# Ranking tokens within their experts by sums over fours of token tiles instead of single tiles

## The chip, the cores and the metric

The kernel runs on one NeuronCore of a Trainium2 chip. The metric is the device time of one execution in microseconds (us), as the median of the runs. The engines are TensorE (PE: matrix products; its weight loads are listed apart as PEld), VectorE (DVE), ScalarE (ACT), GpSimd (POOL) and SyncE (SP), which issues most DMA transfers. Each runs its own instructions in order and waits for others through semaphores.

## The reference

Two layers work on 64 batches of 64 tokens with 1024 features (4096 tokens), each with a residual sum. The first multiplies each batch by one of 16 small matrices and adds a routed low-rank term over 8 experts. The second, cut to what matters:

```
w = weight[adapter_ids];  y = einsum('bij,bkj->bik', x, w)        # a 1024 x 1024 adapter for each batch
base_out = y @ base_w.T + base_b
res_hidden = y @ A.T                                              # 64 wide
logits = y @ router_w.T;  probs = softmax(logits)                 # 16 experts
topw, topi = top_k(probs, 2);  topw = topw / (sum(topw) + 1e-6)
combine = sum(one_hot(topi, 16) * topw)
delta = einsum('bse,bsr,eor->bso', combine, res_hidden, B)
x = x + base_out + delta * 0.5
```

Each token takes two of the 16 experts. The kernel computes an expert's product only for the tokens that chose it, so it must sort the 8192 (token, choice) pairs by expert. The place of a pair within its expert is a count of the tokens ahead of it that chose the same expert.

## The kernel before

Tokens lie on 128 partitions in NT = 32 token tiles of 128 tokens (two batches each). Matrix products in fp32 are written as three products of operands split into a high and a low part (`split_product`, lines 1437 to 1441).

The second layer has these stages. First come the adapter products with `w` (lines 1538 to 1571), which also leave the router logits and the 64-wide hidden values in DRAM. Then comes the base product for each token tile, `base_part(t, n)` (line 1575): 16 parts a tile, three products of 512 columns each, with `xp_hi` and `xp_lo` as weights and `base_hi` and `base_lo` as moving operand. One tile's `xp_hi` and `xp_lo` are kept at a time, in four quarters. ACT makes a quarter of `xp_hi` (`y_high`, line 795) when PE has used that quarter of the tile before, and DVE makes the same quarter of `xp_lo` (`y_low`, line 1174) behind it. The order of everything is written out by hand, in one list for each engine.

The routing lies among the first eight base tiles. DVE picks the two experts of each token in `choose_first` and `choose_second` (lines 1197 to 1217). The result is `hot`, 128 tokens x 32 tiles x 16 experts, 1 where the token chose the expert, and `hot_sum`, its sum over the tiles. The semaphore `hot_ready` says that both are there.

After base tile 2, PE runs `rank_sums` (line 1595). All its products add into one PSUM bank of 512 columns (32 tiles x 16 experts). The first, with the strictly triangular matrix `before`, counts the tokens ahead within the same tile. The other 31, with the matrix `ones`, add the whole count of tile t to all later tiles: tile 0 to 31 tiles (496 columns), tile 1 to 30, and so on to 16 columns. A last product of 16 columns sums `hot_sum` over the partitions. It sets `sums_done`.

DVE then weighs the choices (`weigh`), turns the counts into slots (`place`, line 1230, which waits for `sums_done`) and makes the one-hot table `hot_a` (`tile_of_rows`, line 1254) and `hot_b` (`row_of_rows`, line 1261). PE uses these in `row_sums` beside base tile 6 to find each slot's token. POOL gathers the hidden values by those rows, and the expert products follow, mixed with base tiles 8 to 12. The remaining base tiles come after that, with the gathers of the expert results, the final sums and the stores.

DVE's list around the ranking is: `y_low` for tile 2, quarters 2 and 3; `choose_second`; `y_low` for tile 3, quarters 0 and 1; four subtractions of expert weights (`expert_low(6)` and `(7)`, line 1187); `y_low` for tile 3, quarters 2 and 3; `weigh`; the four quarters of tile 4; `place`; the four of tile 5; `tile_of_rows`.

Of the kernel before, what the change touches and what calls it, by code (L numbers as in the profile page):

```python
# [6 lines left out]
F32 = mybir.dt.float32  # L7
F32R = mybir.dt.float32r
# [3 lines left out]
AX = mybir.AxisListType  # L12

P = 128
# [3 lines left out]
E0, R0 = 8, 16  # L18
E1, R1 = 16, 64
# [5 lines left out]
GT = GR // P  # L25
# [8 lines left out]
NT = NB // 2  # L34
# [53 lines left out]
def bcast(ap, axis, n):  # L88
    shape = list(ap.shape)
    shape.insert(axis, n)  # L90
    return ap.unsqueeze(axis).broadcast_to(shape)


def build(nc, xT, id0, id1, w0, p0T, rb0, b0T, w1T, baseT, q1T, bias1, out):
# [6 lines left out]
    ctx = ExitStack()  # L101
    with ctx:
# [3 lines left out]
        def sb(stack, name, shape, dt=F32):  # L106
            return stack.enter_context(nc.sbuf_tensor(name, shape, dt))
# [12 lines left out]
        ones = sb(ctx, "ones", [P, P], F32R)  # L120
# [4 lines left out]
        desc0 = sb(ctx, "desc0", [P, GT, E0])  # L125
        desc1 = sb(ctx, "desc1", [P, E1])
        rbias = sb(ctx, "rbias", [P, E0])
        sm = sb(ctx, "sm", [P, 10, GT, E0])
        sv = sb(ctx, "sv", [P, 8, GT])
        tok = sb(ctx, "tok", [P, NT])  # L130
        gate = sb(ctx, "gate", [P, 2, NT])
        slots = sb(ctx, "slots", [P, 2 * NT], I32)
        rows = sb(ctx, "rows", [P, NX], I32)
# [45 lines left out]
        with ExitStack() as s:  # L179
            lg = sb(s, "lg", [P, NT, E1])  # L180
            rt = sb(s, "rt", [P, 6, NT, E1])
            hot = sb(s, "hot", [P, NT, E1], F32R)
            hot_sum = sb(s, "hot_sum", [P, E1], F32R)
            etab_f = sb(s, "etab_f", [1, NX])
            rv = sb(s, "rv", [P, 9, NT])
            ev = sb(s, "ev", [P, 5, E1])
# [11 lines left out]
        def bank(i, n=1):  # L198
            return psum[:, i * 512:(i + n) * 512]
# [684 lines left out]
        def _(dve):  # L884
# [305 lines left out]
            rl = Chain(dve, route_chain)  # L1190
# [16 lines left out]
            def choose_second():  # L1207
                dve.reduce_max(m2, sh2, AX.X).then_inc(shift2, 1)
                dve.wait_ge(shift2, 1)
                rl(tt(tmp, sh2, bcast(m2, 2, E1), ALU.is_equal))  # L1210
                rl(tt(tmp, tmp, rank, ALU.mult))
                rl(dve.reduce_max(k2, tmp, AX.X))
                rl(tt(oh2, rank, bcast(k2, 2, E1), ALU.is_equal))
                rl(tt(hot[:, :, :], oh1, oh2, ALU.add))
                with nc.allow_low_precision("small whole numbers"):
                    dve.reduce_sum(hot_sum[:, :], hot[:, :, :].bitcast(F32).rearrange("p t e -> p e t"), AX.X
                                   ).then_inc(hot_ready, 1)

            def weigh():
# [84 lines left out]
            y_low(2, 2)  # L1304
            y_low(2, 3)
            choose_second()
            y_low(3, 0)
            y_low(3, 1)
# [86 lines left out]
            for i in range(LAST + 1):  # L1395
                t = KEPT + i
# [12 lines left out]
        def _(pe):  # L1409
            mm = pe.matmul  # L1410
# [184 lines left out]
            def rank_sums():  # L1595


                pe.wait_ge(hot_ready, 1)
                mm(bank(0), before[:, :], hot[:, :, :].rearrange("p t e -> p (t e)"), start=True, stop=False,
                   skip_group_check=True)  # L1600
                for t in range(NT - 1):
                    mm(bank(0)[:, (t + 1) * E1:NT * E1].rearrange("p (t e) -> p t e", e=E1), ones[:, :],
                       bcast(hot[:, t, :], 1, NT - 1 - t), start=False, stop=t == NT - 2, skip_group_check=True)
                mm(bank(1)[:, 0:E1], ones[:, :], hot_sum[:, :], start=True, stop=True).then_inc(sums_done, 1)

            def row_sums(n):
# [20 lines left out]
            def expert_of(s):  # L1627
                return pe.value_load(etab[0:1, s:s + 1], min_val=0, max_val=E1 - 1)
# [21 lines left out]
            for t in range(FIRST):  # L1650
                for n in range(16):
                    base_part(t, n)
                    if t == 0 and n == 1:
                        turn(total)
                    if t == 0 and n == 5:
                        rh_of(total)
                    if t == FIRST - 2 and n % 2 == 1:
                        row_sums(n // 2)
                    if t == FIRST - 1 and n == 13:
                        turn_hw(0)  # L1660
                if t == 2:
                    rank_sums()
            pe.wait_ge(etab_ready, 1)
            pe.wait_ge(exp_lo_done, E1)
            e = expert_of(0)
            for s in range(NX):
                expert(s, e)
                if s + 1 < NX:
                    e = expert_of(s + 1)
# [50 lines left out]
```

## Time and profile before

| | us |
|---|---|
| median of 3 runs | 1165.05 |
| lowest, highest | 1164.32, 1165.34 |
| the profiled execution's own time | 1167.17 |
| its span in the trace | 1165.6 |
| PE busy | 1103.1 (95% of the span) |
| DVE busy | 686.3 (59%) |
| ACT busy | 505.3 (43%) |
| POOL busy | 222.2 (19%) |

The span runs from the first to the last instruction in the trace. The profiled execution took 1.6 us more than its span and 2.1 us more than the median. Products on PE are pipelined: the record of one overlaps that of the next, so what a product costs in a row of them is the distance from its start to the start of the next, not its duration.

### The profile page before, as it was taken

Reading aid. Unit: us, or ns where it says so; the run is one execution under the profiler, and the core shown is the slowest. Engines: PE = TensorE matmul, PEld = TensorE weight load, DVE = VectorE, ACT = ScalarE, POOL = GpSimd, SP = SyncE. Lnnn points to the kernel's source line nnn. Section 1 sums busy time; section 2 is a strip of 40 time slices with the busy share of each in tenths; the row PEclk is TensorE's granted clock in tenths of the full one; section 3 lists DMA queues with packets and bytes.
Section 4 is the critical chain, followed back from the end, with each engine's and each line's share of the span. In section 5 each row is a group of like instructions: output and inputs, shape, how many; then the busy total and the mean of one; then the engine's idle time right before and its main releaser. Section 6 shows DMA issues by size and latency. Waiting matters only on the chain.

```text
span 1165.6 us, 22333 instructions
## 1 busy us (share of the span) xinstructions
PE 1103.1 (95%) x5801; PEld 916.3 (79%) x5802; DVE 686.3 (59%) x1321; ACT 505.3 (43%) x1027; POOL 222.2 (19%) x354
## 2 busy tenths in 40 slices
PE   4899979999999899999999999999999999999998
PEld 4899967878778687878878878767777778888886
DVE  4788943563755637463565486834455366566666
ACT  1012213563745637453565462134555444444443
POOL 1111110020201102010111000054545232223210
PEclk9899979999999899999999999999999999999999
DMA  6499765493765729475665432169999899999995
GB/s 212 169 313 326 258 223 177 136 323 114 256 222 195 266 82 325 153 259 180 221 221 183 137 102 88 57 223 330 345 336 334 315 404 341 348 354 337 324 323 204
DMA packets 114925, 283.11 MB, mean 243 GB/s; under 512 B 17202, under 2 KB 22322, under 8 KB 112946
## 3 DMA queue, kind: packets, MB, share of 16 engines
q1 hardware_dynamic: 85232, 178.95, 43.3%
q0 software_dynamic: 29216, 102.91, 26.0%
q10 hardware_dynamic: 418, 0.53, 0.2%
q8 instruction: 28, 0.46, 0.2%
q14 instruction: 31, 0.25, 0.1%
HBM read 181.65 MB, written 100.70 MB: 242 GB/s over the span
## 4 chain that ended last, share of the span: by engine, by line
PE 74%; DVE 11%; issue 4%; DMA 4%; ACT 3%; DVEq 1%; SPq 1%; ACTq 1%; POOL 0%; POOLq 0%; another core or an unknown queue 0%
PE psum L1439 18%; PE psum L1441 17%; PE psum L1440 17%; PE psum L1533 3%; PE psum L1637 3%; PE psum L1636 3%; PE psum L1525 2%; PE psum L1645 2%; DVE x1g L1045 2%; PE psum L1534 2%; PE psum L1551 2%; PE psum L1553 1%; DMA xp<-act_scratch 1%; PE psum L1449 1%; ACT w L821 1%
## 5 line engine op out<-in xcount | busy, mean ns | idle before, releaser
L1439 PE MATMUL psum<-base_hi,xp_hi 128*128 128x512 f32 x512 | 207.6, 405 | 6.2 <-DVE xp_lo L1177 3.4
L1441 PE MATMUL psum<-base_hi,xp_lo 128*128 128x512 f32 x512 | 200.4, 391 | 0.0
L1440 PE MATMUL psum<-base_lo,xp_hi 128*128 128x512 f32 x512 | 200.2, 391 | 0.0
L1439 PE MATMUL psum<-w,xp_hi 128*128 128x512 f32 x448 | 182.8, 408 | 6.3 <-DVE xp_lo L1095 3.2
L1441 PE MATMUL psum<-w,xp_lo 128*128 128x512 f32 x448 | 177.7, 397 | 0.0
L1440 PE MATMUL psum<-w,xp_hi 128*128 128x512 f32 x448 | 177.3, 396 | 0.0
L1077 DVE TENSOR_TENSOR w<-raw,w 128x1024 fp32r<-128x1024 f32 x112 | 132.4, 1221 | 29.5 <-ACT w L758 23.6
L639 POOL DMA_DIRECT2D raw<-w1T x112 | 59.4, 530 | 442.8 <-DVE w L1077 417.5
L803 ACT ACTIVATE xp_hi<-xp 128x256 fp32r<-128x256 f32 x124 | 51.6, 418 | 183.1 <-PE psum L1441 152.3
L1439 PEld LDWEIGHTS psum<-base_hi,xp_hi 128*128 128x128 f32 x512 | 96.2, 188 | 39.8 <-issue 15.6
L1177 DVE TENSOR_TENSOR xp_lo<-xp,xp_hi 128x256 fp32r<-128x256 f32 x124 | 51.9, 424 | 119.3 <-ACT xp_hi L803 96.5
L1441 PEld LDWEIGHTS psum<-base_hi,xp_lo 128*128 128x128 f32 x512 | 96.1, 188 | 20.8
L647 POOL DMA_INDIRECT hwn<-rh_scratch,rows x80 | 76.0, 951 | 184.3 <-DVE rows L1274 115.8
L1440 PEld LDWEIGHTS psum<-base_lo,xp_hi 128*128 128x128 f32 x512 | 96.4, 188 | 16.8
L1439 PEld LDWEIGHTS psum<-w,xp_hi 128*128 128x128 f32 x448 | 84.4, 188 | 26.8 <-issue 9.2
L758 ACT ACTIVATE w<-raw 128x1024 fp32r<-128x1024 f32 x104 | 104.6, 1052 | 0.0
L1441 PEld LDWEIGHTS psum<-w,xp_lo 128*128 128x128 f32 x448 | 84.3, 188 | 20.5
L1440 PEld LDWEIGHTS psum<-w,xp_hi 128*128 128x128 f32 x448 | 84.7, 189 | 17.8
L868 ACT ACTIVATE x1t<-x1t,bias 128x128 f32<-128x128 f32 x256 | 78.6, 390 | 12.7 <-DMA x1t<-act_scratch 12.7
L1095 DVE TENSOR_TENSOR xp_lo<-xp,xp_hi 128x512 fp32r<-128x512 f32 x58 | 40.0, 690 | 70.9 <-ACT xp_hi L710 70.5
L1109 DVE COPY yp<-psum 128x512 f32 x28 | 19.4, 691 | 96.2 <-PE psum L1441 95.9
L720 ACT ACTIVATE yp<-psum 128x512 f32 x28 | 16.8, 599 | 136.1 <-PE psum L1441 135.9
(278 smaller groups left out, 1993.5 us busy)
## 6 DMA issues: line engine op xcount, KB each, us to landing
raw<-w1T POOLq DMA_DIRECT2D x120, 512.0 KB, 5.6
delta_scratch<-dl SPq DMA_DIRECT2D x80, 512.0 KB
xp<-act_scratch SPq DMA_DIRECT2D x74, 256.0 KB, 3.3
act_scratch<-yT SPq DMA_DIRECT2D x72, 256.0 KB, 2.2
act_scratch<-x1g SPq DMA_DIRECT2D x16, 1024.0 KB, 5.3
x1t<-act_scratch SPq DMA_DIRECT2D x64, 256.0 KB
out<-x1t SPq DMA_DIRECT2D x62, 256.0 KB
xg<-xT SPq DMA_DIRECT2D x15, 1024.0 KB, 8.6
```

The lines of the kernel that those rows point to most:

```text
L639: pool.dma_start(raw[:, i, :], w1T[bass.ds(a, 1), i, :, :].rearrange("a p k -> p (a k)")).then_inc(raw_in[i], 16)
L647: pool.indirect_dma_start(hwn[s % HRING][:, :], None, rhs[0:NB, :, :].rearrange("b c z -> (b c) z"), bass.IndirectOffsetOnAxis(ap=rows[:, ...
L758: act.activation(w_hi[:, i, :], raw[:, i, :], ACT.Copy).then_inc(w_hi_done, 1)
L803: act.activation(xp_hi[:, ks, :].rearrange("p i (b c) -> p b i c", b=2), xp[:, t % 2, :, ks, :], ACT.Copy).then_inc(yh_done, 1)
L868: last = act.activation(x[:, :, i, :], x[:, :, i, :], ACT.Identity, bias=bias[:, i:i + 1])
L1077: tt(w_lo[:, i, :], raw[:, i, :], w_hi[:, i, :].bitcast(F32), ALU.subtract).then_inc(w_lo_done, 1)
L1095: tt(xp_lo[:, ks, :].rearrange("p i (b c) -> p b i c", b=2), xp_of(j, total, ks), xp_hi[:, ks, :].bitcast(F32).rearrange("p i (b c) -> p b ...
L1177: tt(xp_lo[:, ks, :].rearrange("p i (b c) -> p b i c", b=2), xp[:, t % 2, :, ks, :], xp_hi[:, ks, :].bitcast(F32).rearrange("p i (b c) -> ...
L1439: mm(out, a_hi, b_hi, start=start, stop=False, skip_group_check=True)
L1440: mm(out, a_hi, b_lo, start=False, stop=False, skip_group_check=True)
L1441: return mm(out, a_lo, b_hi, start=False, stop=stop, skip_group_check=True)
L1533: mm(rh_ps, yq_hi[:, i, :], q2[:, i, :], start=i == 0, stop=False, skip_group_check=True)
```

## The change

`rank_sums` now goes by fours of tiles. Three products, each over all eight fours at once, add a tile's count to the tiles d = 1, 2 and 3 places on within its four: they read 8 pieces of 48, 32 or 16 columns out of `hot` and write 8 such pieces with gaps between them. Seven products add the count of a whole four to all later tiles: 448, 384 and so on down to 64 columns. The count of a four, `hot_four` (128 x 8 x 16), comes from a new DVE reduction of `hot`, and `hot_sum` is now reduced from `hot_four` in place of `hot`. The temporary tile `sm` of the first layer (10 x 2 x 8 words of 4 bytes for each partition, 640 bytes) now shares its place with tiles that are written later, so the buffers allocated after it lie 640 bytes lower.

```diff
-        sm = sb(ctx, "sm", [P, 10, GT, E0])
         sv = sb(ctx, "sv", [P, 8, GT])
         tok = sb(ctx, "tok", [P, NT])
+        with ExitStack() as s:
+            sm = sb(s, "sm", [P, 10, GT, E0])
         gate = sb(ctx, "gate", [P, 2, NT])
...
             hot = sb(s, "hot", [P, NT, E1], F32R)
+            hot_four = sb(s, "hot_four", [P, NT // 4, E1], F32R)
...
                 rl(tt(hot[:, :, :], oh1, oh2, ALU.add))
                 with nc.allow_low_precision("small whole numbers"):
-                    dve.reduce_sum(hot_sum[:, :], hot[:, :, :].bitcast(F32).rearrange("p t e -> p e t"), AX.X
+                    rl(dve.reduce_sum(hot_four[:, :, :], hot[:, :, :].bitcast(F32).rearrange(
+                        "p (b i) e -> p b e i", i=4), AX.X))
+                    dve.reduce_sum(hot_sum[:, :], hot_four[:, :, :].bitcast(F32).rearrange("p b e -> p e b"), AX.X
                                    ).then_inc(hot_ready, 1)
...
-                for t in range(NT - 1):
-                    mm(bank(0)[:, (t + 1) * E1:NT * E1].rearrange("p (t e) -> p t e", e=E1), ones[:, :],
-                       bcast(hot[:, t, :], 1, NT - 1 - t), start=False, stop=t == NT - 2, skip_group_check=True)
+                fours = NT // 4
+                out = bank(0).rearrange("p (b i e) -> p b i e", i=4, e=E1)
+                for d in range(1, 4):
+                    mm(out[:, :, d:4, :].rearrange("p b i e -> p b (i e)"), ones[:, :],
+                       hot[:, :, :].rearrange("p (b i) e -> p b (i e)", i=4)[:, :, 0:(4 - d) * E1],
+                       start=False, stop=False, skip_group_check=True)
+                for b in range(fours - 1):
+                    mm(bank(0)[:, (b + 1) * 4 * E1:NT * E1].rearrange("p (t e) -> p t e", e=E1), ones[:, :],
+                       bcast(hot_four[:, b, :], 1, (fours - 1 - b) * 4), start=False, stop=b == fours - 2,
+                       skip_group_check=True)
```

The order of PE's instructions before, at the start of `rank_sums` behind base tile 2 (the row gives line, operation, output and inputs, columns, and the semaphore waited for):

```order
L1441 MATMUL psum<-base_hi,xp_lo 128x512
L1599 MATMUL psum<-hot,before 128x512 [waits hot_ready]
L1602 MATMUL psum<-hot,ones 128x496
L1602 MATMUL psum<-hot,ones 128x480
L1602 MATMUL psum<-hot,ones 128x464
L1602 MATMUL psum<-hot,ones 128x448
L1602 MATMUL psum<-hot,ones 128x432
L1602 MATMUL psum<-hot,ones 128x416
```

The list of L1602 goes on in steps of 16 columns down to 16. The same place on PE in the changed kernel, whole, up to the first product of base tile 3:

```order
L1603 MATMUL psum<-hot,before 128x512 [waits hot_ready]
L1608 MATMUL psum<-hot,ones 128x8x48
L1608 MATMUL psum<-hot,ones 128x8x32
L1608 MATMUL psum<-hot,ones 128x8x16
L1612 MATMUL psum<-hot_four,ones 128x448
L1612 MATMUL psum<-hot_four,ones 128x384
L1612 MATMUL psum<-hot_four,ones 128x320
L1612 MATMUL psum<-hot_four,ones 128x256
L1612 MATMUL psum<-hot_four,ones 128x192
L1612 MATMUL psum<-hot_four,ones 128x128
L1612 MATMUL psum<-hot_four,ones 128x64
L1615 MATMUL psum<-hot_sum,ones 128x16
```

Ten products stand where 31 stood. The product ahead of them and the one behind them are the same as before.

DVE before, from the making of `hot` to `weigh`:

```order
L1214 TENSOR_TENSOR hot<-rt 128x512 [waits route_chain]
L1216 TENSOR_REDUCE hot_sum<-hot 128x16 [waits route_chain]
L1177 TENSOR_TENSOR xp_lo<-xp,xp_hi 128x2x2x64 [waits yh_done] x2
L1187 TENSOR_TENSOR w<-raw,w 64x1024 [waits exp_hi_done] x4
L1177 TENSOR_TENSOR xp_lo<-xp,xp_hi 128x2x2x64 [waits yh_done] x2
L1223 TENSOR_REDUCE rv<-rt 128x32 [waits exp1]
```

The same place on DVE in the changed kernel:

```order
L1216 TENSOR_TENSOR hot<-rt 128x512 [waits route_chain]
L1218 TENSOR_REDUCE hot_four<-hot 128x128 [waits route_chain]
L1220 TENSOR_REDUCE hot_sum<-hot_four 128x16 [waits route_chain]
L1179 TENSOR_TENSOR xp_lo<-xp,xp_hi 128x2x2x64 [waits yh_done] x2
L1189 TENSOR_TENSOR w<-raw,w 64x1024 [waits exp_hi_done] x4
L1179 TENSOR_TENSOR xp_lo<-xp,xp_hi 128x2x2x64 [waits yh_done] x2
```

One reduction more stands ahead of `hot_ready` and of all that follows on DVE. Nothing else moved.

## Rows read from the trace of the kernel before

**Rows 1.** The page: busy time, share of the span and instructions of each engine

```profile
PE 1103.1 (95%) x5801; PEld 916.3 (79%) x5802; DVE 686.3 (59%) x1321; ACT 505.3 (43%) x1027; POOL 222.2 (19%) x354
```

**Rows 2.** Busy time of each engine in stretches of the span

```profile
core 0: us, PE busy (x) PEld busy (x) DVE busy (x) ACT busy (x) POOL busy (x), PEclk, DMA share, GB/s
698.00:703.10 5.10, 5.10 (x36) 4.82 (x35) 4.98 (x6) 2.03 (x5) 0.00 (x0) 1.00 0.26 103
758.00:870.00 112.00, 108.22 (x473) 79.78 (x472) 51.88 (x98) 52.69 (x106) 59.01 (x62) 1.00 0.87 306
870.00:1165.60 295.60, 286.36 (x1381) 233.24 (x1379) 175.65 (x267) 131.58 (x379) 79.98 (x82) 1.00 0.92 330
```

**Rows 3.** The chain that ended last, 696 to 740 us: start, us, what

```profile
698.67 4.40 PE psum L1602 x31
...
724.83 0.24 PE psum L1441
...
725.97 5.41 DVE hot_a L1255
```

**Rows 4.** Timeline of PE: start, us, engine, line, operation, shape

```profile
698.28 0.39 PE L1599 MATMUL psum<-hot,before 128*128 128x512 f32 x1
698.51 4.56 PE L1602 MATMUL psum<-hot,ones 128*128 128x496 f32 x31
702.93 0.26 PE L1604 MATMUL psum<-hot_sum,ones 128*128 128x16 f32 x1
703.04 0.48 PE L1439 MATMUL psum<-base_hi,xp_hi 128*128 128x512 f32 x1
```

**Rows 5.** The same timeline in four narrow windows within L1602

```profile
699.98 0.33 PE L1602 MATMUL psum<-hot,ones 128*128 128x384 f32 x1
...
701.21 0.40 PE L1602 MATMUL psum<-hot,ones 128*128 128x256 f32 x2
...
702.07 0.37 PE L1602 MATMUL psum<-hot,ones 128*128 128x128 f32 x2
...
702.48 0.38 PE L1602 MATMUL psum<-hot,ones 128*128 128x64 f32 x2
```

**Rows 6.** Groups of DVE reductions by shape, 695 to 725 us: busy, mean ns

```profile
L1216 DVE TENSOR_REDUCE hot_sum<-hot 128x16 fp32r<-128x512 f32 x1 | 1.0, 1014 | 0.0
...
L1212 DVE TENSOR_REDUCE rv<-rt 128x32 f32<-128x512 f32 x1 | 0.7, 687 | 0.0
...
L1243 DVE TENSOR_REDUCE ev<-rt 128x16 f32<-128x256 f32 x1 | 0.4, 420 | 0.0
```

**Rows 7.** Timelines of DVE and of PE's weight loads around the ranking

```profile
696.76 1.01 DVE L1216 TENSOR_REDUCE hot_sum<-hot 128x16 fp32r<-128x512 f32 x1
...
698.05 0.19 PEld L1599 LDWEIGHTS psum<-hot,before 128*128 128x128 f32 x1
...
703.48 0.76 DVE L1177 TENSOR_TENSOR xp_lo<-xp,xp_hi 128x256 fp32r<-128x256 f32 x2
...
725.54 0.42 DVE L1177 TENSOR_TENSOR xp_lo<-xp,xp_hi 128x256 fp32r<-128x256 f32 x1 [1.22 <-ACT xp_hi L803]
```

**Rows 8.** Timeline where PE waits for DVE ahead of base tile 6

```profile
736.88 1.43 DVE L1177 TENSOR_TENSOR xp_lo<-xp,xp_hi 128x256 fp32r<-128x256 f32 x4
737.41 0.19 PEld L1439 LDWEIGHTS psum<-base_hi,xp_hi 128*128 128x128 f32 x1 [1.91 <-ACT nat L812]
...
737.76 0.39 PE L1440 MATMUL psum<-base_lo,xp_hi 128*128 128x512 f32 x1
```

**Rows 9.** Timeline of PE in the first layer, products of plain f32

```profile
96.44 2.02 PE L1449 MATMUL psum<-p,xg 128*128 128x136 f32 x16
98.20 0.37 PE L1439 MATMUL psum<-h_hi,b_hi 128*128 128x256 f32 x1
```

**Rows 10.** The page: two of its costliest groups on PE

```profile
L1440 PE MATMUL psum<-base_lo,xp_hi 128*128 128x512 f32 x512 | 200.2, 391 | 0.0
...
L1440 PE MATMUL psum<-w,xp_hi 128*128 128x512 f32 x448 | 177.3, 396 | 0.0
```

## The prediction

> **What bounds the kernel now.** I read the page's busy times first. PE is busy for 95% of the span, DVE for 59% [rows 1], so PE work that disappears can count fully, and DVE work only where PE waits for it. Next I asked for busy time by stretches. In the 5.1 us of the ranking PE never stands still, at a granted clock of 1.00; behind it PE is busy for 108.2 of 112 and 286.4 of 295.6 us, while the DMA engines are at 0.87 and 0.92 [rows 2]. Then I read the chain that ended last. It runs through all 31 products of L1602 as one piece of 4.40 us, stays on PE to the end of base tile 4 (724.83), and only then goes to DVE for `hot_a` [rows 3]. So the ranking products are on the path. Last came the timelines, for the price of a product by its size [rows 4, 5] and for how close DVE is behind or ahead [rows 7, 8].
>
> The products as a whole: the first of L1602 starts at 698.51 and the product behind the last at 702.93, 4.42 us for 31 products and 7936 columns [rows 4]. That is 0.143 us each. The new list has 10 products and 2560 columns, a third of both, but the price of a product isn't proportional to its columns, so I split it by size.
>
> **The price by size.** From start to start [rows 4, 5]:
> - 496 to 400 columns (7 products, mean 448): 699.98 - 698.51 = 1.47 us, 0.21 each.
> - 384 to 272 (8, mean 328): 701.21 - 699.98 = 1.23, 0.154 each.
> - 256 to 144 (8, mean 200): 702.07 - 701.21 = 0.86, 0.108 each.
> - 128 to 80 (4): 0.41, 0.10 each. 64 to 16 (4): 702.93 - 702.48 = 0.45, 0.11 each.
>
> So below some 200 columns nothing gets cheaper: a product costs 0.11 us however small. Above it the price rises to 0.21 at 448. I read off between the bands 0.18 at 384, 0.15 at 320, 0.13 at 256, and 0.11 for 192, 128 and 64.
>
> **What the change adds on PE.** The seven products over fours (448 down to 64 columns): 0.21 + 0.18 + 0.15 + 0.13 + 3 x 0.11 = 1.00 us. The three products over d have 8 x 48 = 384, 256 and 128 columns: 0.18 + 0.13 + 0.11 = 0.42 us. Together 1.42 us in place of 4.42: **3.00 us less on PE**.
>
> This takes the three as if they wrote one piece. They write eight pieces of 48, 32 or 16 columns with gaps, and no product of the kernel before does so. The lower bound is 0.42 us. For the upper I take the dearest product per column that the trace has: 16 records of L1449 (8 products of plain f32, two records each) take 98.20 - 96.44 = 1.76 us [rows 9], 0.22 us for 136 columns, 1.62 ns a column. By that 768 columns would cost 1.24 us, 0.82 more. I take the lower value: within a piece the columns lie side by side, the operand types are those of L1602, and L1602 itself reads its moving operand in pieces of 16 columns at the prices above.
>
> The Trainium skill speaks against this (SBUF — State Buffer, section "Door 1: The DMA port swizzle"): it states that PSUM has lines of 8 bytes and that any access to it that isn't contiguous slows matmuls significantly. It gives no factor, and no row here shows such a product. Were each of the three doubled, the sum would be 0.42 us worse.
>
> **What it adds on DVE.** The reduction L1216 took 1.01 us, while one of the same 512 elements that reads them side by side took 0.69 and one of 256 took 0.42 [rows 6]. That is 0.15 fixed and 0.54 for 512 elements read in order; read 16 words apart, 0.15 and 0.86. The new reduction to `hot_four` reads 512 elements, again 16 words apart inside each sum: 1.01 us, and 0.69 at the least. The one to `hot_sum` now reads 128: 0.15 + 0.86 / 4 = 0.37 us, at the least 0.15 + 0.14 = 0.29, at the most 1.01 as before. The instruction gap adds about 0.04. So `hot_ready` comes later by 1.01 + 0.04 + 0.37 - 1.01 = 0.41 us, with bounds of 0.01 and 1.05.
>
> The Trainium skill has a rule for this as well (same page and section): SBUF works in lines of 16 bytes, and a step to a new line at each element costs extra. The trace agrees, 1.01 against 0.69 us [rows 6]. By the rule `hot_four` costs the 1.01 that I take; by the length of the sums alone it would be 0.69, and the wait worked out next would vanish.
>
> **The wait that this makes.** `hot_sum` was done at 696.76 + 1.01 = 697.77 [rows 7]. PE loaded its weights for L1599 at 698.05. From the end of a DVE instruction to a weight load that waits for it takes 0.11 us: the first `xp_lo` of the four ends at 736.88 + 0.42 = 737.30 and the load starts at 737.41 [rows 8]. So the data was usable at 697.88, with a cover of 0.17 us. Now it is usable at 698.29. After such a stall the second product starts 0.35 behind the weight load (737.41 to 737.76) [rows 8], that is at 698.64, where it started at 698.51 [rows 4]. The stall is **0.13 us**; by the bounds of the reductions it is 0 to 0.77 (usable at 698.93, second product at 699.28). Behind the waiting product in PE's queue stands all of base tile 3, so the stall counts fully.
>
> **What is late next.** Base tile 3 would start at 703.04 - 2.87 = 700.17. Its first two quarters of `xp_lo` come just behind the reductions on DVE, by 698.9: in time. Its third quarter stands behind four subtractions of expert weights. It started at 703.48 [rows 7], now 0.41 later, lasts 0.42 and is usable 0.11 behind: 704.42. PE wants it two quarters into the tile, 24 products of 0.23 us [rows 4] after the start: 705.6. Cover 1.2 us. So this limits the gain only above some 4.0 us. `weigh` ends some 0.4 us later, by 706.5, and nothing on PE needs it. `place` waits for `sums_done`, long set, and starts behind the last quarter of tile 4, which moves with PE. DVE stands idle for 1.22 us ahead of 725.54 and is released there by ACT behind PE [rows 7], so the long `hot_a` (5.41 us, on the path [rows 3]) starts earlier by the whole gain too. The wait of PE for DVE at 737.41 [rows 8] starts and ends with the same chain and stays as it is. Row table, gathers, expert products and stores all start behind it.
>
> The smaller move: `hot_four` and the 640 bytes by which the buffers shift. I cost them at nothing: the DMA sizes, queues and counts stay the same.
>
> **The sum.** 3.00 - 0.13 = 2.87 us. The profiled execution, 1167.17 us with a span of 1165.6, would become 1164.3 with a span of 1162.7. The runs' median stands 2.1 us lower at 1165.05 and becomes **1162.2 us**, 0.25% less. What a measurement of this kernel can tell from no change is about 0.2%, here 2.3 us, so the forecast lies just over that.
>
> **Rivals.**
> - *The gap-writing products and the wait are dear.* The three products at 1.62 ns a column give 0.82 us back, a wait at its upper bound 0.64 more. Gain 2.05 with the first alone, 1.4 with both: 1163.0 to 1163.6 us, within 0.2%. For it: no row shows such a write, and the page cited has a rule against it. Against: both bounds are far from the nearest rows.
> - *The gain is given back later.* PE is idle for 3.8 + 9.2 = 13 us from 758 on, with the DMA engines at 0.87 to 0.92 [rows 2]. If an earlier start only meets transfers that end when they did, and these waits grow by 2 us, the time is 1164.2. For it: the DMA share. Against: every transfer of these stretches is released by the chain that moves.
> - *Slower by the layout.* `base_hi`, `base_lo`, `xp` and `raw` lie 640 bytes lower; `w` stays. Products of one form cost differently by where they read: records of 391 ns with `base`, 396 with `w` [rows 10]. If the shift costs each of the 1536 base products (3 x 512) those 5 ns, that is 7.7 us: 1165.05 - 2.87 + 7.7 = 1169.9. It eats the gain from 1.9 ns a product on and is slower by over 0.2% from 3.4 ns on. Against: nothing ties the 5 ns to the address rather than to what else ran then.
> - *The products aren't fewer.* The order of instructions shows 10 in place of 31, so this has no chance worth giving.
>
> **How the numbers follow.** Forecast (gain 2.4 to 3.3) 0.62; dear writes or wait 0.15; given back 0.17; layout 0.06. The forecast lies near the limit of 0.2% and the runs spread by 0.5 us to each side, so 0.05 of its 0.62 counts as "same", and 0.03 of the first rival as "faster". Faster 0.57 + 0.03 = 0.60; same 0.05 + 0.12 + 0.17 = 0.34; slower 0.06. The range goes from 1161.3 (full 3.0 and a low median) to 1164.2 (most of the gain given back).
>
> **What would show it.** In the changed profile: ten products between L1603 and L1615 with about 1.4 us from the first start to L1615's; the three of L1608 at 0.18, 0.13 and 0.11 from start to start (the first rival: 0.2 us and more each); two reductions of 1.0 and 0.37 us and a weight load of L1603 that starts 0.1 us behind the second; base tile 3 some 2.9 us earlier, and `hot_a` too; PE's idle time from then on the same 13 us (more in the second rival); the 512-column records of the base products at 391 ns (the third: 396). The prediction is wrong if the 2.9 us at tile 3 don't arrive, or if they do and the end doesn't move with them.

## The result, and the profile after

The changed kernel takes 1159.72 us (median of 19 runs, 1155.03 to 1164.31); the kernel before, run alongside, 1164.32 us (19 runs, 1160.98 to 1168.26). The ratio is 0.9958 with a 95% interval of 0.9945 to 0.9972: 4.9 us less, between 3.3 and 6.4. The forecast was 2.9 us less, so the direction is right and the gain is 2.0 us too small. The time lies below the range that I gave (1161.3 to 1164.2).

Read first the stretch that the change touches. The page after, busy time of each engine (as rows 1):

```profile
PE 1100.2 (95%) x5780; PEld 913.8 (79%) x5781; DVE 686.6 (59%) x1322; ACT 504.1 (43%) x1027; POOL 221.4 (19%) x354
```

PE is busy for 2.9 us less with 21 instructions less [rows 1]. The timeline of DVE, PE's weight loads and PE around the ranking, after (as rows 4 and 7: start, us, engine, line, operation):

```profile
698.87 1.06 DVE L1218 TENSOR_REDUCE hot_four<-hot 128x128 fp32r<-128x512 f32 x1
699.96 0.37 DVE L1220 TENSOR_REDUCE hot_sum<-hot_four 128x16 fp32r<-128x128 f32 x1
...
700.39 0.19 PEld L1603 LDWEIGHTS psum<-hot,before 128*128 128x128 f32 x1 [0.28 <-DVE hot_sum L1220]
700.39 0.50 PE L1603 MATMUL psum<-hot,before 128*128 128x512 f32 x1
...
700.73 0.52 PE L1608 MATMUL psum<-hot,ones 128*128 128x384 f32 x3
...
701.08 1.14 PE L1612 MATMUL psum<-hot_four,ones 128*128 128x448 f32 x7
...
702.05 0.26 PE L1615 MATMUL psum<-hot_sum,ones 128*128 128x16 f32 x1
...
702.16 0.48 PE L1443 MATMUL psum<-base_hi,xp_hi 128*128 128x512 f32 x1
```

From the first product of the ranking to that of `hot_sum` it was 702.93 - 698.28 = 4.65 us [rows 4]; now it is 702.05 - 700.39 = 1.66. That is 2.99 us less, and every profile of the study with the new products has 1.65 to 1.67, every one with the old 4.65 to 4.69.

This stretch begins 2.11 us later on the clock (700.39 against 698.28), which the change did not cause: in this execution the first loads landed 0.9 us later, and more of the early work fell into stretches of half clock. So everything below is compared with the ranking's own start, or between many profiles, and the total by the medians of the runs. The busy times in stretches (columns as in rows 2), after:

```profile
core 0: us, PE busy (x) PEld busy (x) DVE busy (x) ACT busy (x) POOL busy (x), PEclk, DMA share, GB/s
700.40:702.10 1.70, 1.70 (x13) 1.64 (x12) 1.67 (x3) 1.53 (x4) 0.00 (x0) 1.00 0.00 0
758.00:870.00 112.00, 109.42 (x481) 81.28 (x480) 53.33 (x100) 53.93 (x108) 59.89 (x64) 1.00 0.88 316
870.00:1161.90 291.90, 282.89 (x1370) 231.09 (x1368) 174.15 (x265) 129.48 (x377) 77.72 (x80) 1.00 0.92 329
```

PE stands still for 2.6 + 9.0 = 11.6 us from 758 on, where it was 13.0 [rows 2]. The chain that ended last, after, around the ranking and on to the one-hot tables (start, us, what):

```profile
700.53 0.36 PE psum L1603
700.89 0.35 PE psum L1608 x3
701.24 0.97 PE psum L1612 x7
...
723.95 0.24 PE psum L1445
...
725.09 5.41 DVE hot_a L1259
```

DVE's timeline just ahead of it, after:

```profile
724.66 0.43 DVE L1179 TENSOR_TENSOR xp_lo<-xp,xp_hi 128x256 fp32r<-128x256 f32 x1 [1.22 <-ACT xp_hi L805]
```

`hot_a` starts at 725.09 where it was 725.97 [rows 3]. That is 0.88 us earlier although the ranking began 2.11 later: the 2.99 us arrive whole, and DVE is idle ahead of it for the same 1.22 us [rows 7]. So the forecast held up to here, and some 1.9 us of the gain come from somewhere else. The page's groups don't show where. After:

```profile
L1445 PE MATMUL psum<-base_hi,xp_lo 128*128 128x512 f32 x512 | 200.0, 391 | 0.0
L1444 PE MATMUL psum<-base_lo,xp_hi 128*128 128x512 f32 x512 | 199.9, 390 | 0.0
...
L1444 PE MATMUL psum<-w,xp_hi 128*128 128x512 f32 x448 | 177.8, 397 | 0.0
L1445 PE MATMUL psum<-w,xp_lo 128*128 128x512 f32 x448 | 177.5, 396 | 0.0
```

Almost nothing moves here [rows 10]: a record holds a product's whole pass, 0.39 us, while the next one starts 0.23 us later. What counts on a full PE is the distance from start to start. I took it from the trace for every pair of neighbouring 512-column products outside the stretches of half clock and call it the spacing. Means in ns, some 1,250 to 1,300 pairs in the adapter stage, 800 in the last base stage, 190 among the experts:

| | adapter (`w` with `xp_hi`, `xp_lo`) | base, tiles 0 to 7 | base, last stage | expert |
|---|---|---|---|---|
| before | 234.1 | 227.3 | 228.1 | 233.4 |
| after | 233.3 | 227.3 | 227.6 | 232.1 |

0.8 ns each over the 1344 adapter products that come in threes is 1.1 us, 0.7 ns over the 256 that come in twos (L1551 and L1553 before) 0.2, 0.45 ns over the 915 base products of the last stage 0.4, about 1 ns over 320 expert products 0.3: together 2.0 us. None of these products is touched by the change. Of the buffers that they read, all but `w` have moved by 640 bytes.

### The profile page after: what moved, and what is told of

Its sections match the earlier page's. It is cut to its first block, busy times and chain, and to the rows that moved or that the text cites. A ratio compares the mean times of both kernels' runs of the same rounds, so it can differ in the third digit from the quotient of the medians.

```text
span 1161.9 us, 22292 instructions
## 1 busy us (share of the span) xinstructions
PE 1100.2 (95%) x5780; PEld 913.8 (79%) x5781; DVE 686.6 (59%) x1322; ACT 504.1 (43%) x1027; POOL 221.4 (19%) x354
## 4 chain that ended last, share of the span: by engine, by line
PE 67%; DVE 11%; DMA 8%; issue 5%; ACT 3%; SPq 3%; DVEq 1%; ACTq 1%; POOL 0%; POOLq 0%
PE psum L1443 16%; PE psum L1444 15%; PE psum L1445 15%; PE psum L1537 3%; PE psum L1647 3%; PE psum L1648 3%; DMA xp<-act_scratch 3%; PE psum L1529 2%; DVE x1g L1047 2%; PE psum L1538 2%; PE psum L1656 2%; DMA out<-x1t 2%; PE psum L1555 1%; PE psum L1453 1%; ACT w L823 1%
## 5 line engine op out<-in xcount | busy, mean ns | idle before, releaser
L1445 PEld LDWEIGHTS psum<-w,xp_lo 128*128 128x128 f32 x448 | 84.4, 188 | 20.6
```

Source lines behind the costliest of these rows:

```text
L1445: return mm(out, a_lo, b_hi, start=False, stop=stop, skip_group_check=True)
```

## The experiments

**The two parts alone.** Each kernel does one part of the change; a repeat of each whole kernel ran with them on one chip. `layout_only` keeps the 31 products and moves the buffers:

```
-        sm = sb(ctx, "sm", [P, 10, GT, E0])
...
+        with ExitStack() as s:
+            sm = sb(s, "sm", [P, 10, GT, E0])
...
+            hot_four = sb(s, "hot_four", [P, NT // 4, E1], F32R)
```

> The kernel before with the new placing of buffers alone (sm shares its place, hot_four allocated and not used); the 31 products stay. If the move of the buffers by 640 bytes is what gave the gain beyond 2.9 us: 1.5 to 2.5 us faster than before (ratio 0.998). If the whole gain comes from the shorter ranking and what follows from it: no difference, ratio 1.000 within 0.1%, and the stretch from the first expert product on shows the same pauses of ACT and DVE as before.

`fours_old_layout` has the ten products and both reductions; `sm` stays where it was, and `hot_four` lies in memory that `hot_a` uses later, so that nothing shifts:

```
+            hot_four = sb(s, "hot_four", [P, NT // 4, E1], F32R)
+        with ExitStack() as s:
             held = [sb(s, f"held{i}", [P, D]) for i in range(HELD)]
```

> The new products and reductions with the buffers where they were before (sm in its own place, hot_four in memory that hot_a uses later). If the gain is that of the products: the full gain of the changed kernel, 3 to 5 us (ratio 0.996 to 0.9975). If the layout gave 2 of it: 2.9 us at most, ratio 0.9975. In the profile base tile 3 starts 3.0 us earlier against the product ahead of the ranking in either case.

The repeats, without an edit:

> The changed kernel once more, beside the two others. If the gain beyond 2.9 us was chance of the runs: ratio 0.9975 (2.9 us). If it is real: 0.996 (4.7 us). Its profile is a second one: if the two microseconds at the first expert products are systematic, PE passes from the first product of L1647 to the fifteenth products later without the waits of the kernel before; if chance, they may be there.

> The kernel before, unchanged, run as if it were a variant. It shows what a ratio of two equal kernels looks like (1.000 within 0.15%), and gives a second profile: if the pauses of ACT and DVE behind the first expert products (2 us of PE's time between 770 and 779) belong to the kernel before, they stand in it again; if they are chance, they are shorter or gone.

Measured against the kernel before (12 runs each, 35 of the kernel before): the ten products alone 0.9973 (0.9956 to 0.9989), which is 3.1 us (1.3 to 5.1); the move alone 0.9977 (0.9956 to 0.9997), which is 2.7 us; the change again 0.9959 (0.9943 to 0.9975); the kernel before again 1.0002 (0.9983 to 1.0020). The part that I had forecast is worth what I said (2.9) within that interval, and the interval of the part that I had costed at nothing (0.3 to 5.1 us) only just leaves out zero. The spacing is the sharper measure, and it goes with the move alone: 233.29 ns in the adapter stage with the old products and the new places, 234.11 with the new products and the old places.

**Is it the place within 512 bytes?** `xp_hi`, `xp_lo`, `base_hi`, `base_lo`, `raw` and `xg` begin 480 bytes past a multiple of 512 in the kernel before and 352 past one after. `layout_again` repeats the move; `shift_512` adds 128 bytes to it, so that the buffers lie 512 bytes off and within 512 bytes as before; the last two put both kernels' buffers on a multiple of 512:

```
shift_512 (on layout_only)   +        pad = sb(ctx, "pad", [P, 32])
before_aligned               +        pad = sb(ctx, "pad", [P, 8])
change_aligned               +        pad = sb(ctx, "pad", [P, 40])
```

> The kernel with the new placing of buffers and the 31 old products, a second time. The first time it was 0.9977 of before. If the placing really gives some 2.3 us: 0.998 again, at most 0.999. If that was chance of twelve runs: 1.000 within 0.15%.

> As the layout kernel (old products), but with 128 bytes of padding behind etab, so that the buffers lie 512 bytes lower than before and not 640: every large buffer starts 480 bytes past a multiple of 512, as before. If the gain of the placing comes from where rows start within 512 bytes (480 before, 352 in the change): no gain here, 1.000, and the 576-byte DMA packets of rh_scratch take 37.5 ns as before. If it comes from sm's own place or from the mere distance: 0.998, as with 640 bytes.

> The kernel before with 32 bytes of padding behind etab, nothing else: every large buffer starts on a multiple of 512 bytes. If the start within 512 bytes is what the placing changed: 0.997 to 0.998 of before. If it is not: 1.000.

> The changed kernel with 160 bytes of padding behind etab: every large buffer starts on a multiple of 512 bytes. If the start within 512 bytes counts, a row of 2048 bytes then lies in four such pieces and not in five, and this is faster than the changed kernel by 1 us or more, 0.995 of before. If it doesn't count: the same as the changed kernel, 0.996.

Measured: `layout_again` 0.9987 (0.9973 to 1.0000), `shift_512` 0.9993 (0.9979 to 1.0008), `before_aligned` 0.9963 (0.9946 to 0.9980), `change_aligned` 0.9932 (0.9913 to 0.9951). The runs of two kernels overlap too much for 1 us, but the spacing is sharp: in the adapter stage 233.29, 234.10, 232.60 and 232.56 ns. With the old place within 512 bytes the old spacing is back. So the place decides, not the distance moved, and not the new tile. The groups of `before_aligned` show a little of it:

```profile
L1442 PE MATMUL psum<-w,xp_lo 128*128 128x512 f32 x448 | 176.9, 395 | 0.0
L1441 PE MATMUL psum<-w,xp_hi 128*128 128x512 f32 x448 | 176.7, 394 | 0.0
```

**Which buffer?** Two theories stood: the target of the weight loads by DMA (`raw`), whose writes would disturb PE's reads, and the operands of PE themselves. Both next kernels are the kernel before with 32 bytes added, behind `raw` in the one (only `xp_hi`, `xp_lo` and what follows are moved onto a multiple of 512) and ahead of it in the other (`raw` as well). `base_hi` and `base_lo` stay at 480.

```
         raw = sb(ctx, "raw", [P, KC, D])
+        pad = sb(ctx, "pad", [P, 8])
         xp_hi = sb(ctx, "xp_hi", [P, KC, P], F32R)
```

> The kernel before with 32 bytes of padding behind raw: raw, base_hi, base_lo and xg stay 480 bytes past a multiple of 512, xp_hi, xp_lo, xp, yT, nat and rhl start on one. What counts is the mean distance from start to start of the adapter products (512 columns, back to back, full clock), 234.1 ns in the kernel before and 232.6 with everything aligned. If the transfers into raw (56 MB beside those products) are what slows PE by their place: still near 234.1. If it is the place of xp_hi and xp_lo, PE's weights, or of the small transfers: near 232.6.

> The kernel before with 32 bytes of padding ahead of raw: raw and all behind it start on a multiple of 512 bytes, base_hi, base_lo and xg stay 480 past one. If raw's place counts: adapter products 232.6 ns apart, while the kernel with the padding behind raw has 234.1. If the place of what PE reads (base_hi, base_lo) counts in the last stage: base products there stay at 228.0 ns; if only the transfers' targets count: 227.3.

One run each: 1167.30 and 1165.14 us, beside 1164.19 for the kernel before (median of 12). The adapter products got faster in both (232.58 and 232.62 ns), so `raw` has no part in it. A single run can't tell kernels this close apart, the spacing can. And the base products got slower, which neither theory had: 233.2 ns in tiles 0 to 7 and 233.0 in the last stage, in both kernels. The groups of `pad_behind_raw`:

```profile
L1442 PE MATMUL psum<-base_hi,xp_lo 128*128 128x512 f32 x512 | 202.5, 396 | 0.0
L1441 PE MATMUL psum<-base_lo,xp_hi 128*128 128x512 f32 x512 | 202.3, 395 | 0.0
```

Records of base products now have the 396 ns that [rows 10] shows for `w` alone, and 95 products of base tile 3 and its neighbours become 92 in the same 21 us, at the same clock and DMA share. Busy time in one stretch (columns as in rows 2), the kernel before:

```profile
703.50:724.50 21.00, 21.00 (x95) 17.38 (x94) 12.75 (x33) 3.92 (x9) 0.00 (x0) 1.00 0.22 76
```

The same of `pad_behind_raw`:

```profile
703.50:724.50 21.00, 21.00 (x92) 16.93 (x91) 12.02 (x32) 3.90 (x9) 0.00 (x0) 1.00 0.22 76
```

In every kernel with fast base products, `base` and `xp` lie at the same place within 512 bytes; here they lie 32 bytes apart. `w` has always lain at 128, apart from `xp`. That made a new theory: what counts is the distance between the two operands.

**Distance, or a multiple of 512?** `all_aligned` puts `w` too on a multiple of 512 (384 bytes at the front, padding of 288). `same_place` leaves `w` at 128 and moves all others to 128, so nothing is on a multiple of 512 but the distance is nil. Both are the change with `hot_four` in memory that `hot_a` uses later. `change_aligned_again` stands beside them.

```
all_aligned   +        front = sb(ctx, "front", [P, 96])
both          +        pad = sb(ctx, "pad", [P, 72])
```

> The changed kernel with every large buffer on a multiple of 512 bytes, those at the front too (w, and the buffers of the last stage ga, gb, fin and x1t, which lay 128 bytes past one), and hot_four in memory that hot_a uses later. If transfers whose rows start on such a multiple disturb PE less, the last stage gains again: its base products from 227.3 to about 227.0 ns, some 0.5 us, 0.993 of before. If not: the same as the kernel with the back part aligned.

> The changed kernel with the large buffers on multiples of 512 bytes, a second time: 0.993 to 0.994 of before if the first result (six runs) holds, 0.996 if it was the changed kernel's own.

> The changed kernel with all large buffers behind w, xp_hi and base_hi among them, 128 bytes past a multiple of 512, as w is; hot_four lies in memory that hot_a uses later. If the place of the weights against the moving operand counts: adapter products (w with xp) 228.4 ns apart, as with everything aligned, base products 227.4, and 0.992 of before. If a start on a multiple of 512 counts: adapter products 233 to 234 ns, 0.996.

Measured: `all_aligned` 0.9918 (0.9898 to 0.9937), 1154.33 us; `same_place` 0.9916 (0.9890 to 0.9942), 1155.17 us; `change_aligned_again` 0.9940 (0.9918 to 0.9962). The spacing of the adapter products is 228.39 ns in both of the first two and 232.57 in the third. It is the distance. What I had expected of `all_aligned`, base products at 227.0 ns, did not come (227.6 in the last stage); its gain is that of the adapter products. Groups of `same_place`:

```profile
L1447 PE MATMUL psum<-w,xp_lo 128*128 128x512 f32 x448 | 175.3, 391 | 0.0
L1446 PE MATMUL psum<-w,xp_hi 128*128 128x512 f32 x448 | 174.6, 390 | 0.0
```

The 5 ns between `base` and `w` in [rows 10] have gone. In the timeline of PE it can be read from the starts. The kernel before, where the last row starts 8 products behind the first:

```profile
420.28 0.40 PE L1440 MATMUL psum<-w,xp_hi 128*128 128x512 f32 x1
...
422.15 0.40 PE L1439 MATMUL psum<-w,xp_hi 128*128 128x512 f32 x1
```

`same_place`, where it starts 11 products behind:

```profile
419.72 0.39 PE L1445 MATMUL psum<-w,xp_hi 128*128 128x512 f32 x1
...
422.21 0.39 PE L1447 MATMUL psum<-w,xp_lo 128*128 128x512 f32 x1
```

1.87 / 8 = 0.234 us, and 2.49 / 11 = 0.226.

**Other distances, and the old products.** `apart_64` and `apart_256` are `same_place` with `pad` of 88 and 8 words: all others 64 and 256 bytes (within 512) from `w`. `old_products_same_place` is the kernel before with the places of `same_place`.

> The same with the buffers behind w at 192 bytes past a multiple of 512, so that xp_hi lies 64 bytes from w's place within 512 and at the same place as base_hi. By the relative place: base products 227.4 ns, adapter products between 228.4 (distance 0) and 234.1 (distance 352 or -160). By absolute alignment: both as in the kernel before.

> The same at 384 bytes past a multiple of 512: xp_hi lies 256 bytes from w's place. By the relative place: base products 227.4, adapter products another value than 234.1, 233.3 and 232.6, which were seen at distances of 352, 224 and -128. By absolute alignment: as in the kernel before.

> The 31 old products, without hot_four, with the buffers behind w all 128 bytes past a multiple of 512, as w is. By the relative place: adapter products 228.4 ns apart and not 234.1, 1344 of them, 7.7 us, and the expert products 3 ns less, 320 of them, 1 us; less what DVE and ACT then make late, so 6 to 8.5 us, ratio 0.993 to 0.995. If the place matters only together with the new ranking: 0.998 or more.

Measured: spacings of 233.37, 228.35 and 228.35 ns; times of 1159.83 and 1157.36 us (one run each), and 1158.98 us for the third (9 runs, 0.9940, 0.9919 to 0.9960). 256 bytes are as good as none, where I had expected another value, and 64 as bad as 96 or 224. The expert products, whose moving operand is `w` and whose weights `hwh` and `hwl` always lay at `xp`'s place within 512, follow in the third: 229.9 ns, where they had 233.4. The groups of `apart_64`:

```profile
L1447 PE MATMUL psum<-w,xp_lo 128*128 128x512 f32 x448 | 176.9, 395 | 0.0
L1446 PE MATMUL psum<-w,xp_hi 128*128 128x512 f32 x448 | 176.9, 395 | 0.0
```

And of `apart_256`:

```profile
L1447 PE MATMUL psum<-w,xp_lo 128*128 128x512 f32 x448 | 175.3, 391 | 0.0
L1446 PE MATMUL psum<-w,xp_hi 128*128 128x512 f32 x448 | 174.6, 390 | 0.0
```

All adapter spacings by the distance from `w` to `xp` within 256 bytes:

| distance | 0 | 64 | 96 | 128 | 224 |
|---|---|---|---|---|---|
| kernels | all_aligned, same_place, apart_256, old_products_same_place | apart_64 | before, fours_old_layout, shift_512 | the aligned pair, the padded pair | after, layout_only |
| ns | 228.35 to 228.39 | 233.4 | 234.1 | 232.6 | 233.3 |

The small transfers were a rival too, since they answer to the place as well: the 4608 DMA packets of 576 bytes took 38.0 ns on average at 480 bytes past a multiple of 512, 33.3 at 352 and 30.6 at 0. But `same_place` has 33.7, as good as the 33.3 of the changed kernel, with adapter products 5 ns closer together. So they don't set the spacing.

The spacing overstates what is gained in time. From the first adapter product to the last it was 500.4 us at distance 96 (mean of four profiles, 499.3 to 502.1), 500.2 at 224 (499.7 to 500.7) and 492.9 at 0 (491.6 to 494.7). At 0 that is 7.5 us less where the spacings over 1600 products make 9; at 224 it is 0.2 less where they make 1.3. Between 12.8 and 17.1 us of each of these stages ran at half clock, so half a microsecond can't be told here.

The places alone are worth 0.0060 (0.9940), 7.0 us (4.7 to 9.5), with the old products, where the spacings alone would make some 10; ten products in place of 31 on top give 0.9916. The best version is the change with `w` and `xp` at the same place: 0.9916 and 0.9918, 9.5 to 9.8 us less than the kernel before and 4 to 5 us less than the change.

## Why the prediction was right, and where it failed

**The price by size: the sum right, partly by luck.** The new products took, from start to start, 1.66 us from L1603 to L1615, in which the second started 0.34 behind the first. The seven over fours took 702.05 - 701.08 = 0.97 us, forecast 1.00. The three that write with gaps took 701.08 - 700.73 = 0.35, forecast 0.42. But the floor of 0.11 us "however small" did not hold: 192, 128 and 64 columns took 0.10, 0.08 and 0.08 us, and the last with gaps 0.06, while the first of 448 columns took 0.26 in place of 0.21. These misses cancel. What sets the floor is open.

**Dear gap writes (chance 0.15): refuted.** The three together took 0.35 us; by the starts in the trace they came 0.18, 0.12 and 0.06 us ahead of the next one, the cheapest being the 128 columns in eight pieces of 16. The contiguous ones of the same 384, 256 and 128 columns in the same trace took 0.19, 0.12 and 0.08. The first rival had 0.2 and more for each. The Trainium skill's rule (SBUF — State Buffer, section "Door 1: The DMA port swizzle") that any PSUM access that isn't contiguous slows matmuls significantly is not borne out for pieces of 16 to 48 fp32 columns.

**The reductions: right.** `hot_four` took 1.06 us (forecast 1.01) and `hot_sum` 0.37 (0.37).

**The wait: right.** PE's weight load at 700.39 waits for `hot_sum`, done at 700.34. The second product came at 700.73; with a product's usual distance in this run from the one before it would have been 700.61, so the stall is 0.12 us (forecast 0.13). Here two small misses cancel: the reductions put `hot_sum` 0.05 us later than forecast, and the way from its end to the weight load is 0.05 us in place of 0.11.

**What is late next: nothing, right.** From the first L1604 before and L1615 after, to the first product with `hot_a`, 36.66 us passed in both; from there to the first expert product 28.55 in both. (PE wanted the third quarter of tile 3 at 700.17 + 24 x 0.23 = 705.7, not 705.6; nothing hangs on it.)

**Given back later (0.17): refuted.** The expected 13 us of idle PE became 11.6, not 15; over nine profiles with the old products and nine with the new, PE is idle behind 758 us for 12.4 and 11.7 us on average (10.3 to 14.5 and 10.1 to 13.3). There is a little of the opposite. Between the last store of expert results and the first gather, the chain that ended last reads, before (start, us, what):

```profile
919.04 0.61 ACT dl L855
919.71 4.59 DMA delta_scratch<-dl
924.37 0.71 issue
925.08 0.94 POOL ga L658
```

And after:

```profile
915.60 0.61 ACT dl L857
916.26 2.81 DMA delta_scratch<-dl
919.14 0.71 issue
919.85 0.95 POOL ga L660
```

From the store's issue to the gather it is 5.4 us before and 3.6 after. All nine profiles with the new products have 3.5 to 3.6, all nine with the old 4.6 to 5.4, whatever the places. So it is no chance. But it hardly shows at the end: from the start of the last expert product to the end of the span the nine have 245.0 to 248.0 us (mean 247.1), and the old without the two slow padded kernels 245.3 to 249.9 (mean 247.5). The products alone gave 3.1 us in the runs (1.3 to 5.1), 0.1 more than the ranking accounts for. What shortens that wait, and what takes it back, I did not find.

**The failed step: "The smaller move ... I cost them at nothing".** The reason I gave, that DMA sizes, queues and counts stay, looks at the wrong reader. The third rival did ask whether products cost differently by where their operands lie, and set 5 ns on it, but it had three faults. It allowed for slower only, though nothing in the profile gave a sign. It looked at the base products, whose two operands move together and which stayed at 227.3 ns in tiles 0 to 7; the adapter and expert products, whose moving operand `w` stays while their weights move (`xp_hi` and `xp_lo`, `hwh` and `hwl`), were left out. And it dismissed the 5 ns because "nothing ties the 5 ns to the address rather than to what else ran then"; `same_place` and `pad_behind_raw` tie them to it in both directions. What should have stood in the sum is a term of unknown sign: by [rows 10] up to 5 ns on 1600 adapter and 320 expert products, some -10 to +10 us. What the runs show in its place is a gain of 2.0 us by the spacings, which is rather too much; the two measurements of the move alone gave 2.7 us (0.3 to 5.1) and 1.5 us (0 to 3.2). With the 3.1 us of the products alone this fits the 4.9 us measured.

**The range.** It ended at 1161.3, "full 3.0 and a low median", and so held no gain from outside the ranking. With the term above on both sides it would have reached down to about 1152.

**The profiled pair.** It shows 1167.17 and 1163.52 us, 3.65 less, and the parts are not the medians' parts: 2.1 us lost ahead of the ranking and 1.9 us won in the first expert products. The latter is a pause of PE, in the timeline before:

```profile
770.93 0.50 PE L1636 MATMUL psum<-w,hwh 128*128 x1 [0.30 <-DVE dl L1338]
...
773.27 0.49 PE L1636 MATMUL psum<-w,hwh 128*128 x1 [0.73 <-ACT dl L855]
```

From the first expert product to the 41st passed 20.75 us there, but 18.8 in the repeat of the same kernel and 18.9 after. So the same kernel has it or not. Of the nine profiles with the old products five have it (20.6 to 21.6 us), of the nine with the new one (20.6); the others have 18.8 to 19.0. That may be chance; if it isn't, it is worth under 1 us on average and part of what the ten products gave. It was not tried further.

**Still open.** The last base stage went from 228.1 to 227.6 ns with the move (228.0 to 228.1 in all four kernels at the old places, 227.3 to 227.6 in all others where `base` and `xp` have equal places). Its operands move together, so the distance between them doesn't explain it. And I did not try places finer than 32 bytes, nor `xp_hi` and `xp_lo` apart from each other.

## What to carry to other kernels

When a change shifts buffers, write down where each operand of the hot loop lies before and after, even if the change is about something else, and give the shift a term with both signs. Where PE is full and each product loads new weights, read the distance from start to start instead of the record's length, compare it between loops, and if one loop is 2% slower at the same shape, try its two operands at the same place within 256 bytes. To credit a gain to its cause, run each part alone: here the total looked like one gain and was two of different kinds.

## What the hardware showed that I had not expected

- A pair of weight load and 512-column product took 228.4 ns when weights and moving operand lay at the same place within 256 bytes and 232.6 to 234.1 at the four other distances tried (adapter stage, with its 1344 products); for the base products of tiles 0 to 7 227.3 to 227.6 against 233.2 at 32 bytes. The Trainium skill says (TensorE: Matmul & The Clock Gate, section "Step-by-step: what each phase is for") that TensorE reads weights and moving operand by two independent ports, and that the load of the next weights takes no bandwidth from the running product. The spacings here differ by the distance between the two, at full clock and with the same instructions, which two reads that have nothing to do with each other wouldn't do. That both share something which the distance decides is argued from this, not shown.
- Products that write PSUM in pieces with gaps cost no more than others: 0.35 us for the three of 384, 256 and 128 columns, where the prices of the products before gave 0.42. Contiguous ones of the same sizes took 0.39 in the same trace. Why small products took 0.06 to 0.10 us here and 0.11 before [rows 5] was not tried.
- From the end of `hot_sum` on DVE to the weight load that waits for it passed 0.05 us; I had taken 0.11 from `xp_lo` [rows 8].
